# A relational graph layer on one core: eleven tiles of messages fetched row by row instead of 29, a head of 520 tiles, and x for the end loaded in pieces

## The chip, the core and the metric

The kernel runs on one core of one Trainium2 chip. The metric is the device time of one execution in microseconds (us); the time before is the median of three executions.

## The reference

x has 12,500 nodes of 64 features. There are 200,000 edges, each with a source, a destination, one of 64 relations and a weight; the edges are sorted by destination, and low node numbers have many edges. With h = relu(layernorm(x)) the result is:

```python
W   = einsum('rb,bio->rio', comp, basis)              # 64 matrices of 64 x 64
msg = h[src] * norm
s   = segment_sum(msg, etype * N + dst)              # per relation and node
y   = relu(einsum('rni,rio->no', s, W) + bias) + relu(h @ res_w.T + res_b)
out = x + (y - mean(y)) * rsqrt(var(y) + BN_EPS) * gamma + beta   # mean and var over nodes
```

## The kernel before

The edges lie in 1,563 tiles of 128. They are treated in two ways.

**The table.** Since a message times a matrix is linear, the kernel first computes the products of every node with all 64 matrices and writes them to device memory (`z_table`, 205 MB): TensorE (PE) multiplies (L1132), ScalarE (ACT) empties PSUM into `zst` (L578), SyncE (SP) stores 1 MB at a time (L441). When it has landed, the edge tiles from 512 on (1,051 of them) need one row of 64 numbers for each edge. Each such table tile is gathered, then PE multiplies it with a one-hot matrix `oh`, which VectorE (DVE) builds from destinations and weights (L1009), so that one matmul (L1248) adds 128 rows into a window of nodes; four tiles make a unit, and DVE adds its window to `acc` (L991). `s_agg` counts the tiles multiplied.

**The head.** The first `HEAD` = 512 tiles (the nodes with the most edges) don't use the table. GpSimd (POOL) gathers their raw x rows while the table is being written (L528), SP stores them eight tiles at a time to `head_rows`, and later they are read back: DVE and ACT normalize them (L1020 to L1035, L687, L700, L701; L1022 subtracts the means of eight tiles), PE multiplies with a one-hot of (node, relation) (L1040, L1262), DVE adds to `sacc` (L1001), and each of six chunks ends in 32 matmuls with the matrices (L1271, "relations"). The list `sums` spreads the head's items between the table tiles 4 to 855 in a fixed order, which PE, DVE and ACT all follow.

**Who gathers table tiles.** POOL gathers 1,022 of them, one indirect DMA each (L555), into a ring of 36 buffers (`ys`, NY = 36): gather q waits until the tile of gather q - 36 has been multiplied. SP fetches 20 tiles and ACT 9, each as 128 single-row DMAs (`fetch`, L394), into three buffers each. SP takes a tile after each 50 gathers (`SP_EVERY`). `owner` is the table of who fetches what.

**The end.** `acc` holds the sums of node pairs in two halves. The epilogue has 13 chunks of 1,024 nodes (512 columns; the last 128): PE adds the halves (`sum_halves`, L1206), ACT adds the bias and takes the relu (`shifted`, L655), DVE adds the residual part and takes statistics (`moments`, L927, L929). Eleven chunks are done early, between late table tiles (`DONE`, `EPI_EARLY`); chunks 11 and 12 come behind the last tile. Then come the statistics over all nodes (L1061 and on), ACT scales each chunk (L728), PE transposes it back (L1088), DVE adds x (L1082, `xo`, a view of `zst`), SP stores it (L498). `zst` is also where `sacc` lies, so SP loads x only when the relations are through (`s_rel`) and, in program order, when all its rows are fetched: one DMA of 3 MB and one small one (L490, L493).

Of the kernel before, what the change touches and what calls it, by code (L numbers as in the profile page):

```python
# [6 lines left out]
F32 = mybir.dt.float32  # L7
I32 = mybir.dt.int32
# [5 lines left out]
P = 128  # L14
# [3 lines left out]
GT = 8  # L18
# [13 lines left out]
HEAD = 512  # L32
# [3 lines left out]
HEAD_ENDS = (209, 296, 362, 418, 467, HEAD)  # L36
# [10 lines left out]
WINS = (36, 40, 46, 50, 54, 60, 64, 68, 72, 76, 82)  # L47
# [3 lines left out]
DONE, DONE_STEP = ((176, 9), (187, 11)), 5  # L51
# [3 lines left out]
SP_EVERY, SP_FIRST, NSP = 50, 58, 3  # L55
ACT_BATCH, ACT_REST, ACT_EPI, ACT_TILES, NACT = 14, 64, 10, 9, 3
ACT_LATE = 30


def rgcn_kernel(nc, x, src, dst, etype, weight, basis, comp, bias, res_w, res_b, gamma, beta, out):  # L60
# [15 lines left out]
    HR = HEAD // HC  # L76
# [5 lines left out]
    assert LE < UT * P and 2 * UT * P == GE  # L82
    assert 64 < GB <= GA <= P and HEAD % GT == 0 and HEAD % HB == 0 and HR <= P and len(WINS) * WIN_BLOCK == NGZ

# [9 lines left out]

    chunk_of = [sum(t >= end for end in HEAD_ENDS) for t in range(HEAD)]
# [14 lines left out]
    assert epi_after == sorted(epi_after) and epi_after[-1] + NOH + 1 < NZT  # L110
# [29 lines left out]
    tile_at_factor, tile_now = [], 0  # L140
    for kind, t, *_ in sums:
        if kind == "tile":
            tile_now = t
        elif kind == "factor":
            tile_at_factor.append(tile_now)

    def tile_of_row(n):

        if n < ACT_BATCH * NHB:
            return tile_at_factor[n // ACT_BATCH]  # L150
        return HEAD_UNTIL + (n - ACT_BATCH * NHB) * 0.36

    owner, pooled, nsp, nact = {}, 0, 0, 0
    for u, tiles in enumerate(units[:-NU]):
        pooled += len(tiles)
        if u % NU < NU - 1:
            continue
        if nact < ACT_TILES and unit_end[u] >= tile_of_row((nact + 1) * P - 1) + ACT_LATE:
            owner[unit_end[u]] = ("act", nact)
            nact += 1  # L160
            pooled -= 1
        elif pooled >= SP_FIRST + SP_EVERY * nsp:
            owner[unit_end[u]] = ("sp", nsp)
            nsp += 1
            pooled -= 1
    assert nact == ACT_TILES
    tiles_of_queue = {q: [t for t in sorted(owner) if owner[t][0] == q] for q in ("sp", "act")}
    pool_tiles = [t for t in range(NZT) if t not in owner]
    pool_nth = {t: q for q, t in enumerate(pool_tiles)}
    for a in range(NACT, ACT_TILES):  # L170
        assert tiles_of_queue["act"][a - NACT] < tile_of_row(a * P)
# [6 lines left out]
    with ExitStack() as ctx:  # L178
# [25 lines left out]
        def rest(size):  # L204
# [13 lines left out]
        act_rows = fetched[:, NSP * F:(NSP + NACT) * F].rearrange("p (s f) -> p s f", f=F)  # L218
# [4 lines left out]
        xdup = shared[:, 2 * BANK + 2 * LNT * F:4 * BANK + 2 * LNT * F].rearrange("p (s t a f) -> p s t a f", s=2, a=2, f=F)  # L223
        base_h, span_h = (acc[0:1, k * HEAD:(k + 1) * HEAD] for k in range(2))
# [23 lines left out]
        hlo_f, hhi_f = (wgt_all[:, HEAD + k * HC * P:HEAD + (k + 1) * HC * P] for k in range(2))  # L248
        hspan = sb("hspan", [P, 2, HC])
        off_i = sb("off_i", [1, HEAD], I32)  # L250
# [60 lines left out]
        s_act = [sem(f"s_act{k}") for k in range(NACT)]  # L311
# [11 lines left out]
        s_e1, s_eh, s_ey, s_bst, s_st, s_sc, s_o, s_oc, s_out = (  # L323
            sem(n) for n in ("s_e1", "s_eh", "s_ey", "s_bst", "s_st", "s_sc", "s_o", "s_oc", "s_out"))
# [83 lines left out]
        def _(e):  # L408
# [8 lines left out]
            for arr, to in ((dst, dst_i), (src, src_i), (etype, ety_i), (weight, wgt_f)):  # L417
# [3 lines left out]
                e.dma_start(to[64:GB - 1, 1, :], arr[g1 + 64 * GE:(NG - 1) * GE].rearrange("(g n) -> g n", n=GE)).then_inc(s_zin, 16)  # L421
# [5 lines left out]
            def store_head(b):  # L427
                e.wait_ge(s_hg[b % NRING], 16 * HB * (b // NRING + 1))
                e.dma_start(hd[b, :, :], ring[:, b % NRING, :, :].rearrange("p i f -> p (i f)")).then_inc(s_hst[b % NRING], 16)

# [883 lines left out]
```

## Time and profile before

| | |
|---|---|
| time, three executions | 1994.21, 1989.40, 1991.76 us; median 1991.76 |
| the profiled execution | 1994.12 us, of which the span of its instructions is 1992.1 us |
| busy | PE 1604.7 us, POOL 1479.3, ACT 927.1, DVE 923.4 |
| mean granted TensorE clock | 0.729 |

Times are read from the span's start. "x128" at a row's end means 128 instructions merged into one row; a bracket gives the idle time of the engine ahead of the row and what ended it. SPq and ACTq rows are DMA issues of SP and ACT. The time of a POOL gather is the time in which POOL works on it; its data land later.

### The profile page before, as it was taken

What the parts mean: (1) busy time and instruction counts of PE and PEld (TensorE: products, weight loads), DVE (VectorE), ACT (ScalarE), POOL (GpSimd) and SP (SyncE); (2) the same over time, 40 slices, a digit from 0 to 9 for tenths busy, and PEclk for the clock granted to TensorE, in tenths of its full rate; (3) what the DMA queues carried; (4) which work ended last, traced back from release to release, by engine and by line L of the source; (5) the groups of instructions that cost most, each with busy time, mean ns of one, the idle gap of its engine ahead of it and who ended that gap; (6) DMA issues with size and microseconds to landing.
All of it is one profiled execution on the core that took longest, in us unless ns stands there. A gap on an engine that the chain in (4) does not pass through costs nothing. (4 is left out here: it accounts for less than half of the span.)

```text
span 1992.1 us, 36246 instructions
## 1 busy us (share of the span) xinstructions
PE 1604.7 (81%) x6504; PEld 820.8 (41%) x6553; DVE 923.4 (46%) x3200; ACT 927.1 (47%) x2171; POOL 1479.3 (74%) x1548
## 2 busy tenths in 40 slices
PE   4599999999989858988878798888888989845444
PEld 4243444433333335655544453443444434322222
DVE  6631111311100057887846683783856848424223
ACT  4587777777777465555524442452424424000002
POOL 6777777777777677777777777777777777777773
PEclk9999999999999655555566557568667585856556
DMA  9599999999999522222221221221221211111114
GB/s 189 205 401 405 405 406 399 405 405 405 406 401 403 182 43 49 49 55 50 55 39 38 49 49 33 44 55 32 46 44 38 49 33 38 29 27 28 28 27 141
DMA packets 121905, 308.05 MB, mean 155 GB/s; under 512 B 51100, under 2 KB 51319, under 8 KB 96358
## 3 DMA queue, kind: packets, MB, share of 16 engines
q1 hardware_dynamic: 59822, 236.64, 30.4%
q0 software_dynamic: 49088, 50.36, 12.5%
q10 hardware_dynamic: 12768, 18.71, 3.4%
q14 instruction: 169, 1.38, 0.2%
q8 instruction: 58, 0.95, 0.2%
HBM read 79.75 MB, written 225.83 MB: 153 GB/s over the span
## 5 line engine op out<-in xcount | busy, mean ns | idle before, releaser
L555 POOL DMA_INDIRECT shared<-z_table,idx_all x1022 | 982.8, 962 | 320.4 <-issue 237.1
L528 POOL DMA_INDIRECT acc<-in_x,idx_all x512 | 494.3, 965 | 162.8 <-issue 155.8
L1132 PE MATMUL zps<-wp,res 128*128 128x512 bf16 x2303 | 524.4, 382 | 41.6 <-ACT zst L578 28.9
L578 ACT ACTIVATE zst<-zps 128x512 f32<-128x512 f32 (+1 forms) x784 | 411.3, 602 | 149.8 <-DMA z_table<-zst 127.0
L1132 PEld LDWEIGHTS zps<-wp,res 128*128 128x128 bf16 x2352 | 219.0, 98 | 341.3 <-ACT zst L578 99.4
L1262 PE MATMUL mps<-res 128*128 128x160 f32 (+4 forms) x684 | 347.1, 611 | 11.8 <-issue 6.3
L700 ACT ACTIVATE res<-res,hw 128x64 f32<-128x64 f32 x512 | 176.3, 344 | 302.2 <-DVE hw L1035 118.5
L1009 DVE TENSOR_SCALAR shared<-iota,rel_all,wgt_all 128x36 f32<-128x36 f32 (+10 forms) x1051 | 312.5, 324 | 1.1 <-issue 0.9
L1248 PE MATMUL aps<-shared 128*64 128x36 f32 (+10 forms) x1030 | 193.3, 314 | 123.7 <-DVE shared L1009 57.7
L1248 PE MATMUL zps<-shared 128*64 128x36 f32 (+10 forms) x1014 | 188.7, 313 | 98.6 <-DVE shared L1009 40.5
L1248 PEld LDWEIGHTS aps<-shared 128*64 128x64 f32 x1030 | 126.6, 191 | 298.2 <-issue 199.2
L1248 PEld LDWEIGHTS zps<-shared 128*64 128x64 f32 x1014 | 125.4, 192 | 268.6 <-issue 181.2
L803 DVE SCALAR_TENSOR_TENSOR shared<-zps,res 128x512 f32<-128x512 f32 (+1 forms) x25 | 17.0, 678 | 400.5 <-ACT res L607 400.5
L1262 PEld LDWEIGHTS mps<-res 128*128 128x128 f32 x684 | 168.6, 305 | 45.3 <-issue 10.8
L1271 PE MATMUL zps<-zst,res 128*64 128x256 f32 x384 | 179.3, 607 | 0.0
L1040 DVE TENSOR_SCALAR res<-iota,rel_all 128x160 f32<-128x160 f32 (+4 forms) x512 | 172.8, 338 | 0.2 <-issue 0.2
L1262 PE MATMUL zps<-res 128*128 128x160 f32 (+4 forms) x340 | 172.0, 608 | 0.5 <-issue 0.3
L701 ACT ACTIVATE res<-res,hw 128x64 f32<-128x64 f32 x512 | 170.2, 332 | 0.0
L1001 DVE TENSOR_TENSOR zst<-zst,mps 128x160 f32 (+4 forms) x342 | 124.5, 364 | 78.4 <-PE mps L1262 73.2
L661 ACT ACTIVATE zst<-ones 128x2048 f32<-128x2048 f32 x24 | 43.8, 1895 | 152.2 <-PE zps L1271 152.2
L1020 DVE TENSOR_REDUCE hm<-res 128x8 f32<-128x512 f32 x64 | 43.8, 685 | 103.2 <-DMA res<-head_rows 94.4
L1262 PEld LDWEIGHTS zps<-res 128*128 128x128 f32 x340 | 83.8, 305 | 16.7 <-issue 1.0
(152 smaller groups left out, 881.4 us busy)
## 6 DMA issues: line engine op xcount, KB each, us to landing
z_table<-zst SPq DMA_DIRECT2D x194, 1024.0 KB, 9.6
wp<-z_table SPq DMA_DIRECT2D x2560, 0.2 KB
wp<-z_table ACTq DMA_DIRECT2D x1152, 0.2 KB
head_rows<-acc SPq DMA_DIRECT2D x64, 256.0 KB, 9.9
shared<-z_table,idx_all POOLq DMA_INDIRECT x1022, 2.5
res<-head_rows ACTq DMA_DIRECT2D x62, 256.0 KB
acc<-in_x,idx_all POOLq DMA_INDIRECT x512, 6.2
zst<-in_x SPq DMA_DIRECT2D x1, 3072.0 KB
```

The source lines that it names most:

```text
L528: e.indirect_dma_start(out=ring[:, b % NRING, i, :], out_offset=None, in_=x, in_offset=bass.IndirectOffsetOnAxis(ap=idx_all[:, t:t + 1], a ...
L555: e.indirect_dma_start(out=ys[:, q % NY, :], out_offset=None, in_=table[:, :], in_offset=bass.IndirectOffsetOnAxis(ap=idx_all[:, col:col + ...
L578: e.activation(to, frm, ACT.Copy).then_inc(s_ez, 1)
L700: e.activation(ab[:, t % NABS, 0, :], hs[:, n % 2, i, :], ACT.Identity, scale=hw[:, n % 2, i, 0:1])
L701: e.activation(ab[:, t % NABS, 1, :], hs[:, n % 2, i, :], ACT.Identity, scale=hw[:, n % 2, i, 1:2]).then_inc(s_hab, 1)
L1001: e.tensor_tensor(win, win, head_psum(t)[:, 0:w], ALU.add).then_inc(s_hadd, 1)
L1009: e.tensor_scalar(oh[:, t % NOH, 0:w], iota[:, 0:w], rel_all[:, col:col + 1], wgt_all[:, col:col + 1], ALU.is_equal, ALU.mult).then_inc(s_ ...
L1040: e.tensor_scalar(hoh[:, t % NHOH, 0:w], iota[:, 0:w], rel_all[:, t:t + 1], None, ALU.is_equal).then_inc(s_hoh, 1)
L1132: last = e.matmul(to, lhsT=stationary(px, pw), rhs=moving(px, pw), start=(a == 0), stop=(a == 2))
L1248: e.matmul(unit_psum(u)[h:h + F, 0:w], lhsT=rows, rhs=oh[:, t % NOH, 0:w], start=(k < 2), stop=(k >= size - 2)).then_inc(s_agg, 1)
L1262: e.matmul(head_psum(t)[:, 0:w], lhsT=ab[:, t % NABS, :, :].rearrange("p a f -> p (a f)"), rhs=hoh[:, t % NHOH, 0:w], start=True, stop=Tru ...
L1271: last = e.matmul(zps[0:F, NZB - 1, 0:SUM_NODES], lhsT=wf[:, q, :], rhs=by_relation[:, q, :], start=(q == 0), stop=(q == HALF - 1))
```

## The change

- `HEAD` goes from 512 to 520 tiles. Head indices, destinations, types and weights were loaded as 128 rows of four tiles; the eight new tiles (`MAIN` to `HEAD`) come as four more small DMAs (`xsrc_i`, `xdst_i`, ...), issued by ACT at the start, with small copies on DVE and small transposes on PE beside each that was there.
- DVE writes the head's indices to `idx_all` ahead of its first pass over x rather than behind it, and in two parts, so that POOL waits for the first 64 tiles' indices and then, at tile 64, for the rest (`IDX_FROM`).
- ACT fetches no rows. SP fetches a tile after each 80 gathers, the first after 150: by the planner's rule these are the table tiles 151, 231, 311, 399, 479, 559, 639, 719, 799, 879 and 959, eleven in all. POOL's table gathers become 1,043 - 11 = 1,032, its head gathers 520.
- SP waits for the relations (`s_rel`) ahead of its tenth tile, number 879, and issues x for the end in 13 pieces, one after each 16 rows of its last two tiles.
- `DONE` has a third entry: chunk 11 of the epilogue is done after table tile 1,036. Of the last part, POOL scales chunks 3, 6, 9 and 12, and ACT the other nine.
- A few one-hot windows are two columns wider, the head's chunk bounds are moved, and SP loads one row set less for each of four arrays.

```diff
-HEAD = 512
+HEAD, MAIN = 520, 512
-HEAD_ENDS = (209, 296, 362, 418, 467, HEAD)
+HEAD_ENDS = (212, 301, 368, 425, 475, HEAD)
-DONE, DONE_STEP = ((176, 9), (187, 11)), 5
+DONE, DONE_STEP = ((176, 9), (187, 11), (194, 12)), 5
+POOL_SCALES = (3, 6, 9, 12)
-SP_EVERY, SP_FIRST, NSP = 50, 58, 3
-ACT_BATCH, ACT_REST, ACT_EPI, ACT_TILES, NACT = 14, 64, 10, 9, 3
-ACT_LATE = 30
+SP_EVERY, SP_FIRST, NSP = 80, 150, 3
+X_WITH, X_STEP = 2, 16
...
-                for j, t in enumerate(tiles_of_queue["sp"]):
+                loaded = 0
+                for j, t in enumerate(sp_tiles):
                     if j >= NSP:
-                        e.wait_ge(s_agg, tiles_of_queue["sp"][j - NSP] + 1)
+                        e.wait_ge(s_agg, sp_tiles[j - NSP] + 1)
+                    if j == len(sp_tiles) - X_WITH:
+                        e.wait_ge(s_rel, NHK)
                     for r in range(P):
                         fetch(e, regs, t, r, sp_rows[:, j % NSP, :], s_sp[j % NSP])
-                e.wait_ge(s_rel, NHK)
+                        if j >= len(sp_tiles) - X_WITH and r % X_STEP == X_STEP - 1 and loaded < NEPI:
+                            load_x(loaded)
+                            loaded += 1
...
-            e.wait_ge(s_hidx, 1)
             for t in range(HEAD):
+                if t in IDX_FROM:
+                    e.wait_ge(s_hidx, IDX_FROM.index(t) + 1)
...
+            e.wait_ge(s_st, 9)
+            for n in POOL_SCALES:
+                y = acc[:, n * EPI:n * EPI + epi_width[n]]
+                e.tensor_scalar(y, y, bmv[:, 6:7], bmv[:, 8:9], ALU.mult, ALU.add).then_inc(s_scp, 1)
...
+            e.dma_start(xsrc_i[:, :], extra_rows(src)).then_inc(s_hsrc, 16)
...
+            for to, arr in ((xdst_i, dst), (xety_i, etype), (xlo_f, weight)):
+                e.dma_start(to[0:EX, :], extra_rows(arr)).then_inc(s_hin, 16)
...
-                            fetch_rows(ACT_BATCH * (i + 1) // HB - ACT_BATCH * i // HB)
...
-                fetch_rows(ACT_REST)
                 for n in range(EPI_EARLY):
-                    if n == done_from[1]:
-                        fetch_rows(ACT_TILES * P)
                     shifted(n)
-                    fetch_rows(ACT_EPI)
...
+            e.wait_ge(s_hrow, 1)
+            take_main(idx_all, 0, IDX_FROM[1] // HC).then_inc(s_hidx, 1)
+            take_main(idx_all, IDX_FROM[1] // HC, HR)
+            e.tensor_copy(idx_all[:, MAIN:HEAD], mflat[:, HC * P:HC * P + EX]).then_inc(s_hidx, 1)
```

In the rows below, which give the program's order and no times, a line's number is that of its own version. The first place is the start of ACT's queue, before:

```order
L564 DMA idx_all<-in_src 128x512
L565 DMA comp_sb<-in_L_gnn_comp 64x64
L566 DMA resw_sb<-in_L_gnn_res_w 64x64
L567 DMA resw_sb<-in_L_gnn_res_w 64x64
L568 DMA res<-in_L_gnn_basis 64x4096
L569 DMA rel_all<-in_dst 128x512
L570 DMA rel_all<-in_edge_type 128x512
L571 DMA wgt_all<-in_edge_weight 128x512
```

and with the change:

```order
L563 DMA idx_all<-in_src 128x512
L564 DMA xsrc_i<-in_src 8x128
L565 DMA comp_sb<-in_L_gnn_comp 64x64
L566 DMA resw_sb<-in_L_gnn_res_w 64x64
L567 DMA resw_sb<-in_L_gnn_res_w 64x64
L568 DMA res<-in_L_gnn_basis 64x4096
L569 DMA rel_all<-in_dst 128x512
L570 DMA rel_all<-in_edge_type 128x512
L571 DMA wgt_all<-in_edge_weight 128x512
L573 DMA acc<-in_dst 8x128
L573 DMA acc<-in_edge_type 8x128
L573 DMA acc<-in_edge_weight 8x128
```

One small load (`xsrc_i`) now stands ahead of the loads of comp, res_w and basis, and three more ahead of the biases and of all that ACT computes.

The second place is PE behind the last table tiles (L1248 and L1246 are those tiles, into banks `aps` and `zps`; L1206 and L1208 are `sum_halves`), before:

```order
L1248 MATMUL zps<-shared 64x82 x8
L1248 MATMUL aps<-shared 64x82 x8
L1248 MATMUL zps<-shared 64x82 x7
L1248 MATMUL zps<-shared,wp 64x82
L1248 MATMUL aps<-shared 64x82 x8
L1248 MATMUL zps<-shared 64x82 x3
L1226 UNCONDITIONAL_BRANCH
L1206 MATMUL mps<-acc,stack 64x512 x2
L1206 MATMUL zps<-acc,stack 64x128 x2
```

and with the change:

```order
L1246 MATMUL zps<-shared 64x82 x8
L1246 MATMUL aps<-shared 64x82 x8
L1246 MATMUL zps<-shared 64x82 x5
L1208 MATMUL mps<-acc,stack 64x512 x2
L1246 MATMUL zps<-shared 64x82 x3
L1246 MATMUL aps<-shared 64x82 x3
L1228 UNCONDITIONAL_BRANCH
L1208 MATMUL zps<-acc,stack 64x128 x2
```

The 512-column chunk has moved from behind the last tile to six tiles ahead of it; only the 128-column one is left behind.

The third place is SP's queue where it loads x for the end (`zst<-in_x`), before, behind its last row:

```order
L394 DMA wp<-z_table 1x64
L393 ISA
L394 DMA wp<-z_table 1x64
L467 UNCONDITIONAL_BRANCH
L490 DMA zst<-in_x 128x12x512
L493 DMA zst<-in_x 106x128
L498 DMA out_x<-zst 128x512 x12
```

and with the change, the first of 13 such places, inside tile 879:

```order
L379 DMA wp<-z_table 1x64
L378 ISA
L379 DMA wp<-z_table 1x64
L437 DMA zst<-in_x 128x512
L378 ISA
L379 DMA wp<-z_table 1x64
L378 ISA
```

The load is cut into pieces that stand between rows of the table, the last of them 80 rows into SP's last tile.

## Rows read from the trace of the kernel before

**Rows 1.** The page, part 2: busy tenths of POOL and of DMA in 40 slices.
```profile
POOL 6777777777777677777777777777777777777773
...
DMA  9599999999999522222221221221221211111114
```

**Rows 2.** The page, parts 5 and 6: the two gathers, and issue to landing.
```profile
L555 POOL DMA_INDIRECT shared<-z_table,idx_all x1022 | 982.8, 962 | 320.4 <-issue 237.1
L528 POOL DMA_INDIRECT acc<-in_x,idx_all x512 | 494.3, 965 | 162.8 <-issue 155.8
...
shared<-z_table,idx_all POOLq DMA_INDIRECT x1022, 2.5
```

**Rows 3.** Waits of POOL: engine, line, releaser, us in total, times, longest.
```profile
POOL shared L555 <- issue: 237.1, 777, 0.3
```

**Rows 4.** Timeline of POOL: the first and the last gather from the table.
```profile
668.85 0.94 POOL L555 DMA_INDIRECT shared<-z_table,idx_all  x1 [8.87 <-DMA z_table<-zst]
...
1962.27 0.94 POOL L555 DMA_INDIRECT shared<-z_table,idx_all  x1 [0.30 <-issue]
```

**Rows 5.** POOL in three stretches, the gathers of L555 alone.
```profile
669.00:694.00 25.00, 18.91 (x21) 0.50 0.27 65
860.00:940.00 80.00, 60.93 (x63) 0.50 0.23 51
...
1900.00:1950.00 50.00, 37.81 (x41) 0.51 0.15 27
```

**Rows 6.** Timeline of a stretched gather, 969 to 971 us.
```profile
969.26 0.69 DVE L1022 TENSOR_TENSOR res<-res,hm 128x512 f32<-128x512 f32 x1
...
969.53 1.23 POOL L555 DMA_INDIRECT shared<-z_table,idx_all  x1 [0.30 <-issue]
```

**Rows 7.** Timeline of the DMA queue of SP from 1829 us.
```profile
1829.09 127.33 SPq L394 DMA_DIRECT2D wp<-z_table  x257
1956.79 0.41 SPq L490 DMA_DIRECT2D zst<-in_x  x1
```

**Rows 8.** Timeline behind the last gather: its landing, the last two chunks.
```profile
1968.33 0.54 PE L1248 MATMUL zps<-shared 128*64 128x82 f32 x2 [0.59 <-DMA shared<-z_table,idx_all]
...
1969.35 2.08 PE L1206 MATMUL mps<-acc,stack 128*64 128x512 f32 x4 [0.48 <-DVEq L1055]
...
1971.48 0.69 ACT L655 ACTIVATE acc<-mps,cols 128x512 f32<-128x512 f32 x1 [73.81 <-PE mps L1206]
1972.07 0.36 ACT L655 ACTIVATE acc<-zps,cols 128x128 f32<-128x128 f32 x1
...
1974.15 0.51 DVE L1061 BATCH_NORM_AGGREGATE halves<-bst 128x2 f32<-128x78 f32 x1
```

**Rows 9.** Timeline of the last stretch: DVE adds x to chunks 4 to 12.
```profile
1982.57 5.18 DVE L1082 TENSOR_TENSOR zst<-zst,zps 128x512 f32<-128x512 f32 x9 [0.17 <-PE zps L1088]
```

**Rows 10.** Timeline of the start, and where the stream of products begins.
```profile
4.40 0.45 ACTq L570 DMA_DIRECT2D rel_all<-in_edge_type  x1
...
9.92 1.10 POOL L528 DMA_INDIRECT acc<-in_x,idx_all  x1 [6.97 <-DVE idx_all L746]
...
12.95 0.22 DVE L793 TENSOR_TENSOR shared<-zps,wp 128x64 f32<-128x64 f32 x1 [3.32 <-ACT wp L607]
...
59.17 1.94 PE L1088 MATMUL zps<-ident,shared 128*128 128x128 f32 x8 [13.90 <-DVE shared L773]
```

**Rows 11.** DMA from 60 to 660 us: queue 0, and the gathers issued.
```profile
q0 software_dynamic: 15079, 15.47, 8.5%
...
acc<-in_x,idx_all POOLq DMA_INDIRECT x474, 6.2
```

**Rows 12.** Timeline of PE, the end of the head: relations, then a table tile.
```profile
1731.66 1.02 PE L1271 MATMUL zps<-zst,res 128*64 128x256 f32 x2
...
1736.83 0.50 PE L1248 MATMUL zps<-shared 128*64 128x72 f32 x2 [0.53 <-DMA shared<-z_table,idx_all]
```

**Rows 13.** Timeline of POOL at the start: an operation on 288 columns.
```profile
2.48 0.38 POOL L518 IOTA iota<- 128x288 f32 x1
```

More of the change, by code:

```diff
@@ L109, in rgcn_kernel @@
                  for k in range(len(DONE)) for n in range(done_from[k + 1] - done_from[k])]
-    assert epi_after == sorted(epi_after) and epi_after[-1] + NOH + 1 < NZT
+    moments_at = [min(t + NOH + 1, NZT - 1) for t in epi_after]
+    assert epi_after == sorted(epi_after) and epi_after[-1] < NZT and len(set(moments_at)) == EPI_EARLY
     epi_run = [2 * w // P for w in epi_width]
@@ L137, in rgcn_kernel @@
     assert done == len(head_items)
[L140 to L153, printed above, removed]
+    owner, pooled, nsp = {}, 0, 0
     for u, tiles in enumerate(units[:-NU]):
         pooled += len(tiles)
[L156 to L163, printed above, removed]
+        if u % NU == NU - 1 and pooled >= SP_FIRST + SP_EVERY * nsp:
+            owner[unit_end[u]] = nsp
             nsp += 1
             pooled -= 1
[L166 to L167 removed]
+    sp_tiles = sorted(owner)
     pool_tiles = [t for t in range(NZT) if t not in owner]
     pool_nth = {t: q for q, t in enumerate(pool_tiles)}
[L170 to L171 removed]
     table = nc.dram_tensor("z_table", [NCLS * N * CLS, F], F32)
@@ L429, in store_head @@
                 e.dma_start(hd[b, :, :], ring[:, b % NRING, :, :].rearrange("p i f -> p (i f)")).then_inc(s_hst[b % NRING], 16)
+            regs = [e.alloc_register(f"sp_row{k}") for k in range(REGS)]
             stored = 0
@@ L466, in _ @@
                 e.wait_ge(s_sum, 1)
+                for n in range(NEPI):
+                    load_x(n)
             with e.Else():
@@ L669, in _ @@
                     clear(sacc[:, a:a + 2048]).then_inc(s_flush, 1)
-                e.wait_ge(s_met, 3)
-                regs = [e.alloc_register(f"act_row{k}") for k in range(REGS)]
-                fetched_rows = [0]
-                def fetch_rows(count):
-                    for n in range(fetched_rows[0], min(fetched_rows[0] + count, ACT_TILES * P)):
-                        a, r = divmod(n, P)
-                        if r == 0 and a >= NACT:
-                            e.wait_ge(s_agg, tiles_of_queue["act"][a - NACT] + 1)
-                        fetch(e, regs, tiles_of_queue["act"][a], r, act_rows[:, a % NACT, :], s_act[a % NACT])
-                        fetched_rows[0] = n + 1
                 for kind, n, *_ in sums:
@@ L1282, in _ @@
             for n, w in enumerate(epi_width):
-                e.wait_ge(s_sc, n + 1)
+                pools = sum(k <= n for k in POOL_SCALES)
+                if n in POOL_SCALES:
+                    e.wait_ge(s_scp, pools)
+                else:
+                    e.wait_ge(s_sc, n + 1 - pools)
                 if n >= NZB:
```

141 lines of the change are left out of this document (75 added, 66 removed).

## The prediction

> **What bounds the kernel now.** I read the slices of the page first. POOL shows 7 in nearly every slice from the second to the last but one, while DMA is full in the first third alone [rows 1]. An engine that is 70 to 79% busy all the time may be waiting a little each time or may be full. The groups settle it: 512 head gathers take 494.3 us of work and 162.8 us of gaps, 1,022 table gathers 982.8 and 320.4 [rows 2], and the waits put 237.1 us of those gaps down to "issue", 777 times and never more than 0.3 us [rows 3]. A gather of 0.94 us is followed by a gap of 0.30 [rows 4], also in the 25 us when neither SP nor ACT fetches anything: 18.91 busy of 25.00 is 75.6%, or 0.94 of 1.25 [rows 5]. So POOL issues at its own pace from 9.92 us [rows 10] to 1962.27 us [rows 4], with one real wait, 8.87 us for the table to land [rows 4]. PE is busier in sum, but it is ahead where it counts: when the head's relations end at 1732.7 us it needs 4 us until it waits for a gather's data [rows 12]. The time is POOL's start, its gathers, that one wait, and the tail behind the last gather.
>
> The pace is 1.270 us in the head ((494.3 + 155.8) / 512, without the 7.0 us ahead of the first) and 1.267 at the table ((982.8 + 320.4 - 8.9) / 1022) [rows 2, 4]. The unhindered pace is 1.248, so 1,022 gathers lose 19 us to stretching. What stretches them is seen in one pair of rows: DVE starts L1022, a subtraction with two SBUF inputs, at 969.26 for 0.69 us, and the gather that starts at 969.53 takes 1.23 us instead of 0.94 [rows 6]. From 1900 to 1950 us, with SP fetching rows without a pause [rows 7] and no L1022, the share is 75.6% again; from 860 to 940, with L1022 at work, it is 76.2% [rows 5]. The rows that SP and ACT fetch don't slow POOL; DVE does.
>
> By the Trainium skill (SBUF — State Buffer, section SBUF: two separate sides) DVE and GpSimd share a port pair that the first to start holds for its whole instruction, and a DVE operation with two SBUF inputs takes it against a GpSimd operation that reads SBUF. By that rule, the trace agrees: the stretched gather ends about when it would if it had begun behind L1022. It also says that SP's own DMAs don't take part in this, so by it their removal gives POOL nothing.
>
> **Start.** ACT issues one more DMA ahead of res_w and basis and three more ahead of the biases. Issues follow each other by 0.45 us and a little [rows 10], so four cost 4 x 0.49 = 2.0 us, and all of ACT's work begins 2.0 later. DVE stood 3.32 us waiting for ACT at 12.95 [rows 10], so it is late by the same; the two go on in turns, and PE waits 13.90 us for DVE's product at 59.17, where the stream begins [rows 10]. I take the whole 2.0 as the delay of the stream; the bounds are 0 (all of it absorbed in between) and 2.6. On the other side POOL starts earlier, since its indices are copied ahead of DVE's three operations on x: near 6.8 instead of 9.92.
>
> **The stream and the table's landing.** DMA is at 0.99 there [rows 1], so the stream is as long as its bytes take. Gathers are 8.5% of 16 engines in 600 us, for 474 of them [rows 11]: 0.108 us each, 0.8 for eight more. The table lands 2.0 + 0.8 = 2.8 later, and POOL's first table gather moves from 668.85 to 671.6 (bounds 669 to 673).
>
> **Eight more head gathers** cost 8 x 1.270 = 10.2 us, but they lie in what was the 8.87 us wait: 6.8 + 520 x 1.270 = 667.2, before 671.6. They are free. If POOL started no earlier they would end at 670.3, still before.
>
> **Ten more table gathers** (1,032 for 1,022) have no cover: POOL has no other gap. 10 x 1.267 = **12.7 us** (12.5 at the unhindered pace). The head has one block of eight more, one L1022 more, 0.3 us, which I leave in the range. The last gather starts at 671.6 + 1,031 x 1.267 = 1977.9 instead of 1962.27; I take 2.8 + 12.7 = 15.5 later, 1977.8.
>
> **The tail.** Behind the last gather stand 29.8 us (1962.27 to 1992.1).
> - The last gather's data reached PE at 1968.33, 6.1 us on [rows 8], where 2.5 is the median [rows 2]; SP had issued the 3 MB of x at 1956.79 [rows 7]. With x loaded in pieces 100 us earlier this is 2.5: -3.5 us. Bounds: 0, if something else delayed it, and -3.6.
> - Chunk 11 is no longer behind the last tile. PE's passes begin at 1969.35, ACT's relu of chunk 11 runs at 1971.48, of chunk 12 at 1972.07, and the statistics begin at 1974.15: 4.8 us [rows 8]. With only the 128-column chunk I count 0.75 (PE) + 0.4 (ACT) + 0.6 (DVE's two small operations) + 0.1 = 1.9: -2.9 us (bounds -2.2 to -3.3). Ahead of the last tiles the chunk costs PE 2.08 us, with six gathers or 7.5 us still to come, and these six tiles need 6 x 0.5 [rows 12]: hidden, with some 2 us to spare.
> - POOL's share of the scaling gives nothing. From chunk 4 on DVE works with 0.17 us of idle time ahead, nine chunks in 5.18 us [rows 9]; it, and PE before it, set the pace, not ACT. Does it cost? No row shows this POOL operation. The nearest is 0.38 us for 288 columns [rows 13], so 0.7 for 512 in proportion; the other end is four times that, 2.8. Chunk 3 is wanted three ACT steps of 0.7 in, and then one each 2.1 or more: below 2.1 it is free, at 2.8 the fourth would be 2 to 3 us late. I take 0, being near the lower row.
>
> By the Trainium skill (GPSIMD Engine Reference, section 3.1) a simple one-input operation runs at about 1.03 cycles per element; by it the sum stays as it is.
>
> **Hidden, and what if not.** The rows that SP and ACT no longer issue stood in queues that nobody at the bound waits for. SP's tile 879 is a new risk: its rows are issued only when the relations are through. In the old order that is 1732.7; now I expect 1740 (the 2.8, and eight head tiles more for PE). SP takes 127.33 / 257 = 0.495 us for a row [rows 7], so 128 rows and eight loads of 0.41 take 66.7 us: data at 1807. PE wants this tile when its neighbours land, near 1775, so PE stands for some 30 us. POOL isn't stopped: gather 906 is the first that needs a tile behind 879, it starts at 671.6 + 906 x 1.267 = 1819.5, 12 us later. SP's last tile is in by 1872, wanted at 1876.
>
> **Sum.** 2.8 + 12.7 - 3.5 - 2.9 + 0 = **+9.1 us**. Against the profiled execution: 1994.1 + 9.1 = 2003.2. The median of the runs lies 2.4 below the profiled one, so I forecast 1991.8 + 9.1 = **2000.9 us**, slower by 0.46%. Its own range, from the bounds: 0 to 3.5 at the start, 12.5 to 13.5, -5.8 to -7 in the tail (with -2.2 if the load wasn't to blame), 0 to 2.5 for the scaling, and 3 either way for how DVE's operations happen to meet the gathers: 1995 to 2008.
>
> **Rivals.**
> - *Faster: the stretching goes.* Without ACT's fetches its factors come on time and L1022 falls elsewhere in POOL's cycle. If all 19 us went, the sum would be -10, 1982 us; it decides from 9.1 of 19.3 on, about half. For it: the hits depend on phase. Against it: 65 blocks remain, and row fetches show no effect [rows 5].
> - *Slower still: POOL stops behind tile 879.* Every microsecond that the relations end after 1752 goes to POOL. If they end 20 late, at 1760, it is 8 us, giving 2009. For it: the order of the wait; against it: 12 us of margin.
> - *About the same.* The start's delay is absorbed (-2.8) and fewer gathers are stretched (-3 or more): +3, 1995.
> - *The load of x wasn't what delayed the last data.* Then 3.5 come back: 2004.4, inside the forecast's range.
>
> **Chances.** Forecast with its own range 0.68, stretching goes 0.09, POOL stops 0.08, about the same 0.15. The range of 1992 to 2008.5 leaves out the two outer cases. A measurement of this kernel tells about 0.2% (4 us) from no change: faster by more 0.10, within it 0.16, slower by more 0.74.
>
> **What would show it.** Right: POOL's first head gather before 8 us; its wait for the table 4 to 5 us instead of 8.87, and the first table gather at 671 to 673; 1,032 gathers at 1.267; the last data 2.5 us behind the last gather; PE idle for 25 to 35 us at tile 879 while POOL's waits stay at 0.3. Wrong: a POOL pace under 1.258, a POOL wait of microseconds near 1819, a table that lands before 669.5, or chunks 6, 9 and 12 waiting for POOL.

## The result, and the profile after

The changed kernel takes 2000.73 us in the median of 5 runs (2000.44 to 2004.86), the kernel before, run beside it, 1992.28 us (1989.4 to 1994.21). The ratio is 1.0049, with a 95% interval of 1.0034 to 1.0063: slower by about half a per cent. The forecast was 2000.9 us. The profiled execution of the changed kernel took 2000.53 us with a span of 1998.4, against 1994.1 and 1992.1 before. So the two profiles differ by 6.4 us and the medians by 8.5: the profiled execution of the kernel before lies about 2 us above its median, that of the changed kernel 0.2 below its own.

The lines that answer to [rows 1] and [rows 2], from the page of the changed kernel (L546 is the gather from the table, L519 that of the head):

```profile
POOL 6777777777777777777777777777777777777774
...
DMA  9599999999999522222211221221211211122112
...
L546 POOL DMA_INDIRECT shared<-z_table,idx_all x1032 | 988.7, 958 | 316.1 <-issue 248.1
L519 POOL DMA_INDIRECT acc<-in_x,idx_all x520 | 503.6, 968 | 163.0 <-issue 157.9
```

POOL is the bound as before: 7 in every slice between the ends. What changed is the last digit of DMA, 4 before and 2 now: the 3 MB of x are no longer loaded in the last slice. A table gather is 958 ns on the mean instead of 962, which is less stretching than before; the forecast had it in its range, not in its sum.

The start of the stream of products against [rows 10], then POOL's timeline where the head's gathers end and the table's begin, and at its last gather, against [rows 4]:

```profile
60.78 1.94 PE L1089 MATMUL zps<-ident,shared 128*128 128x128 f32 x8 [13.86 <-DVE shared L770]
...
7.79 1.14 POOL L519 DMA_INDIRECT acc<-in_x,idx_all  x1 [4.84 <-DVE idx_all L733]
...
668.61 0.95 POOL L519 DMA_INDIRECT acc<-in_x,idx_all  x1 [0.30 <-issue]
671.36 0.94 POOL L546 DMA_INDIRECT shared<-z_table,idx_all  x1 [1.80 <-DMA z_table<-zst]
...
1973.34 0.94 POOL L546 DMA_INDIRECT shared<-z_table,idx_all  x1 [0.30 <-issue]
```

The first table gather is 2.5 us later than before and the last one 11.1. Between them are 1,031 steps in 1301.98 us: a pace of 1.263 instead of 1.267. The wait for the table is down to 1.80 us, from 8.87: the eight more head gathers fill nearly all of it.

The tail, against [rows 8] and [rows 9]:

```profile
1970.60 1.21 PE L1208 MATMUL mps<-acc,stack 128*64 128x512 f32 x2
1971.87 0.69 ACT L657 ACTIVATE acc<-mps,cols 128x512 f32<-128x512 f32 x1 [64.75 <-PE mps L1208]
...
1975.86 0.54 PE L1246 MATMUL aps<-shared 128*64 128x82 f32 x2 [0.72 <-DMA shared<-z_table,idx_all]
...
1976.88 0.69 PE L1208 MATMUL zps<-acc,stack 128*64 128x128 f32 x4 [0.48 <-DVEq L1056]
...
1978.65 0.51 DVE L1062 BATCH_NORM_AGGREGATE halves<-bst 128x2 f32<-128x78 f32 x1
1979.21 0.59 PE L1278 MATMUL mps<-halves,wmean 128*128 128x2 f32 x2 [1.64 <-DVE halves L1062]
...
1982.05 6.45 ACT L714 ACTIVATE acc<-acc,bmv 128x512 f32<-128x512 f32 x9 [0.81 <-DVE bmv L1078]
1982.12 2.70 POOL L553 TENSOR_SCALAR acc<-acc,bmv 128x512 f32<-128x512 f32 x4 [7.84 <-DVE bmv L1078]
...
1984.86 9.14 SPq L488 DMA_DIRECT2D out_x<-zst  x13
...
1987.48 5.22 DVE L1083 TENSOR_TENSOR zst<-zst,zps 128x512 f32<-128x512 f32 x9 [0.17 <-PE zps L1089]
```

The last gather's data reach PE 2.5 us behind its start (6.1 before). Chunk 11 passes PE and ACT while gathers are still running, and from the last chunk's pass (1976.88) to the statistics (1978.65) it is 1.8 us instead of 4.8. DVE's nine adds still follow each other with 0.17 us between, 5.22 us against 5.18: relieving ACT by POOL speeds nothing up.

Behind the last gather stand 25.1 us, against 29.8.

### The profile page after: what moved, and what is told of

Read it like the earlier page. It is cut to its first block and busy times, and to the rows that moved or that the text cites. A ratio compares the mean times of both kernels' runs of the same rounds, so it can differ in the third digit from the quotient of the medians.

```text
span 1998.4 us, 29426 instructions
## 1 busy us (share of the span) xinstructions
PE 1633.6 (82%) x6559; PEld 820.3 (41%) x6559; DVE 929.6 (47%) x3234; ACT 902.4 (45%) x2186; POOL 1497.1 (75%) x1570
## 3 DMA queue, kind: packets, MB, share of 16 engines
q0 software_dynamic: 49664, 50.96, 12.7%
## 5 line engine op out<-in xcount | busy, mean ns | idle before, releaser
L546 POOL DMA_INDIRECT shared<-z_table,idx_all x1032 | 988.7, 958 | 316.1 <-issue 248.1
L519 POOL DMA_INDIRECT acc<-in_x,idx_all x520 | 503.6, 968 | 163.0 <-issue 157.9
L1133 PE MATMUL zps<-wp,res 128*128 128x512 bf16 x2352 | 531.9, 382 | 35.2 <-ACT zst L580 26.4
L1246 PE MATMUL aps<-shared 128*64 128x36 f32 (+10 forms) x1040 | 206.8, 314 | 126.0 <-DMA shared<-z_table,idx_all 66.0
L1246 PE MATMUL zps<-shared 128*64 128x36 f32 (+10 forms) x1024 | 204.9, 312 | 107.9 <-DMA shared<-z_table,idx_all 63.2
L1246 PEld LDWEIGHTS aps<-shared 128*64 128x64 f32 x1040 | 133.1, 191 | 323.6 <-issue 154.3
L1246 PEld LDWEIGHTS zps<-shared 128*64 128x64 f32 x1024 | 130.7, 188 | 314.3 <-DMA shared<-z_table,idx_all 154.2
L1269 PE MATMUL zps<-zst,res 128*64 128x256 f32 x384 | 189.1, 611 | 0.0
L992 DVE TENSOR_TENSOR acc<-acc,zps 128x36 f32 (+10 forms) x130 | 28.8, 222 | 142.9 <-PE zps L1246 111.1
L677 ACT ACTIVATE res<-res 128x512 f32<-128x512 f32 x65 | 40.9, 629 | 114.6 <-DVE res L1023 114.1
```

The source lines that it names most:

```text
L519: e.indirect_dma_start(out=ring[:, b % NRING, i, :], out_offset=None, in_=x, in_offset=bass.IndirectOffsetOnAxis(ap=idx_all[:, t:t + 1], a ...
L546: e.indirect_dma_start(out=ys[:, q % NY, :], out_offset=None, in_=table[:, :], in_offset=bass.IndirectOffsetOnAxis(ap=idx_all[:, col:col + ...
L1133: last = e.matmul(to, lhsT=stationary(px, pw), rhs=moving(px, pw), start=(a == 0), stop=(a == 2))
L1246: e.matmul(unit_psum(u)[h:h + F, 0:w], lhsT=rows, rhs=oh[:, t % NOH, 0:w], start=(k < 2), stop=(k >= size - 2)).then_inc(s_agg, 1)
L1269: last = e.matmul(zps[0:F, NZB - 1, 0:SUM_NODES], lhsT=wf[:, q, :], rhs=by_relation[:, q, :], start=(q == 0), stop=(q == HALF - 1))
```

## The experiments

Twelve kernels ran, four at a time on three chips, each four with runs of the kernel before on the same chip. In the first it took 1994.41 us (median of 21), in the second 1994.19 (15), in the third **3092.94** (11). The third chip is a case of its own, and comes last.

**1. How much do the table gathers cost, and do row fetches stretch them?** The kernel before, with nothing but its fetched tiles reduced to eleven, so 1,040 table gathers:

```diff
-SP_EVERY, SP_FIRST, NSP = 50, 58, 3
-ACT_BATCH, ACT_REST, ACT_EPI, ACT_TILES, NACT = 14, 64, 10, 9, 3
+SP_EVERY, SP_FIRST, NSP = 80, 150, 3
+ACT_BATCH, ACT_REST, ACT_EPI, ACT_TILES, NACT = 14, 64, 10, 0, 3
```

> The kernel before with only the table of who fetches changed: SP fetches the same 11 tiles as in the changed kernel, ACT none, so POOL gathers 1,040 table tiles instead of 1,022. Nothing else is different: head of 512, x loaded at the end of SP's list. My theory (POOL's issue pace is all that counts, 1.263 to 1.267 us a gather): +18 x 1.265 = +22.8 us in the gathers. SP is now done with its rows some 70 us before the end, so the 3 MB of x no longer meets the last gather: -3.5. Sum +19.3, a ratio of 1.0097 (1.008 to 1.011). Rival (fetched rows stretch the gathers, so that fewer of them give the time back): the pace falls to 1.248, -19, sum 0, ratio near 1.000.

Measured: 2011.85 us (5 runs), ratio 1.0085 [1.0071, 1.0099], 17.4 us for 18 gathers. Its page and its end:

```profile
L555 POOL DMA_INDIRECT shared<-z_table,idx_all x1040 | 999.5, 961 | 324.0 <-issue 258.1
```
```profile
1984.87 0.94 POOL L555 DMA_INDIRECT shared<-z_table,idx_all  x1 [0.30 <-issue]
```

The mean of 961 ns is that of before (962): without ACT's 1,152 fetches and 1,152 of SP's the gathers are as stretched as with them. 18 gathers at the pace of 1.266 are 22.8 us. The last one's data reached PE 2.7 us behind it instead of 6.25, which gives 3.5 back; SP had issued the load of x at 1744.75 us and not at 1956.79 [rows 7]. The profiles are 19.6 us apart, and the ratio lies in the expected range.

**2. The changed kernel with 20 of SP's tiles (`SP_EVERY, SP_FIRST = 50, 58`), so 1,023 table gathers.**

> The changed kernel with SP fetching a tile after each 50 gathers again, 20 tiles, ACT none: POOL gathers 1,023 table tiles instead of 1,032. My theory: -9 x 1.263 = -11.4 us against the changed kernel, so -2.9 us against the kernel before (2000.7 - 11.4 = 1989.3, ratio 0.9985; 0.997 to 1.000). Rival (the last rows of SP come too late, since SP needs 61 us a tile and has 63): PE waits for SP at the last tile, 1031, and gives 3 to 8 us back.

Measured: 1992.29 us (11 runs), ratio 0.9989 [0.998, 0.9998]. Nine gathers are gone, but SP's last tile is now late; the timeline of PE at the end:

```profile
1967.00 0.40 PE L1246 MATMUL aps<-shared,wp 128*64 128x82 f32 x1 [14.28 <-DMA wp<-z_table]
```

PE stands 14.28 us for a tile from SP, while the last gather had started at 1963.43; the tail is 30.6 us instead of 25.1. The ratio lies in the theory's range, but partly by luck: against the changed kernel the medians are 8 us apart and not 11.4, and the profile shows what the rival named, 5.5 us given back behind the last gather (this execution, 1995.84 us, was the slowest of the eleven). So the fetched tiles pay as long as SP gets through them before the end.

**3. The changed kernel once more, beside the next three on one chip.**

> The changed kernel as it is, to stand beside the other kernels of this call on the same chip. Expected: 1.0049 of the kernel before again, its pace at the table 1.263 to 1.267 us for one gather, and a tail of 25 us behind the last gather.

Measured: 2000.25 us (5 runs), ratio 1.0037 [1.0024, 1.0051]; gathers of 958 ns, pace 1.2624, a tail of 24.9 us.

**4. x loaded whole and late.**

```diff
-                        if j >= len(sp_tiles) - X_WITH and r % X_STEP == X_STEP - 1 and loaded < NEPI:
-                            load_x(loaded)
-                            loaded += 1
-                assert loaded == NEPI
+                e.wait_ge(s_agg, NZT - 7)
+                whole, run = (NEPI - 1) * EPI, epi_run[0]
+                e.dma_start(xoflat[:, 0:whole // P * F].rearrange("p (c r) -> p c r", c=NEPI - 1),
+                            x[0:whole, :].rearrange("(c i j) f -> i c (j f)", c=NEPI - 1, j=run)).then_inc(s_xre, 16 * (NEPI - 1))
+                load_x(NEPI - 1)
```

> The changed kernel with one thing undone: x for the end is loaded in one DMA of 3 MB, and only when seven table tiles are left to sum, so that it runs beside the last gathers, as before the change. Theory (the load of x delayed the last gather's data before): the landing behind the last gather goes from 2.7 us back to about 6, and the time is 3.5 us longer than that of the changed kernel. Rival (something else delayed it, and the load is hidden): the landing stays at 2.7 us and the time is the same.

Measured: 2007.39 us (5 runs), ratio 1.0067 [1.0053, 1.0081]. Its timeline, SP's load and the last gathers (L547) and their products (L1247):

```profile
1968.90 0.43 SPq L482 DMA_DIRECT2D zst<-in_x  x1
...
1974.59 0.94 POOL L547 DMA_INDIRECT shared<-z_table,idx_all  x1 [0.30 <-issue]
1976.63 0.80 PE L1247 MATMUL zps<-shared 128*64 128x82 f32 x4 [3.74 <-DMA shared<-z_table,idx_all]
...
1980.68 0.53 PE L1247 MATMUL aps<-shared 128*64 128x82 f32 x2 [0.40 <-DMA shared<-z_table,idx_all]
```

From the last gather to its product it is 6.1 us again, and to the last of its two products 6.28 against 2.67 in experiment 3: 3.6 us, the theory's number for the landing. The time is another matter: 3.5 us were expected and the medians are 7.1 apart. In the profiles, 5.4 apart, the last gather itself starts 1.8 us later (1974.59 against 1972.78), of which the first table gather's later start is 1.1. What lies beyond the tail's 3.7 isn't explained by the load, and was not looked into by a run.

**5. Chunk 11 late again** (`DONE` without its third entry, `(194, 12)`).

> The changed kernel with chunk 11 of the epilogue behind the last tile again (two entries in DONE). My theory: +2.9 us against the changed kernel (ratio to before 1.0057), seen as 4.8 us instead of 1.8 from the first matmul of sum_halves to the statistics in the profile. Rival (the early chunk costs PE as much ahead of the last tiles as it saves behind): 0.

Measured: 2000.6 us (6 runs), ratio 1.0033 [1.002, 1.0045]. Its last stretch:

```profile
1980.64 0.51 DVE L1062 BATCH_NORM_AGGREGATE halves<-bst 128x2 f32<-128x78 f32 x1
...
1986.12 1.47 DVE L1083 TENSOR_TENSOR zst<-zst,zps 128x512 f32<-128x512 f32 x2 [2.12 <-PE zps L1089]
1986.84 8.13 SPq L488 DMA_DIRECT2D out_x<-zst  x13
1987.76 6.35 DVE L1083 TENSOR_TENSOR zst<-zst,zps 128x512 f32<-128x512 f32 x11 [0.17 <-PE zps L1089]
```

From the last gather's last product to the statistics it is 5.6 us (1975.01 to 1980.64) instead of 2.6 (1976.05 to 1978.65 in the changed kernel): the term of 3 us is there. But the whole tail is 26.2 us, only 1.2 longer than the 25.1 and 1.3 than the 24.9 of the two profiles of the changed kernel. Two things give 1.8 back here. PE's granted clock goes to full at 1988.1 us, 2.0 us behind DVE's first add, and in the changed kernel at 1988.0, 3.9 us behind it. So only one step from add to add takes 0.85 us here and the rest soon 0.60, where the changed kernel has three or four of 0.85; that is 0.6. And the output ends 4.2 us behind the start of SP's last issue, not 5.1; with what SP's queue loses ahead of it that is the other 1.2, and its cause is open (experiment 6). In time the run can't be told from the changed kernel: of the 2.9 us expected none shows.

**6. All scaling by ACT** (`POOL_SCALES = ()`).

> The changed kernel with all 13 chunks scaled by ACT, as before; POOL does nothing behind its last gather. My theory (DVE's additions of x and PE set the pace, not the scaling): no change against the changed kernel, ratio to before 1.004 to 1.005. Rival A (POOL's share gives what it was to give): 1 to 2.5 us slower than the changed kernel, 1.0055. Rival B (POOL at work is why SP's last four issues took 0.5 to 0.66 us instead of 0.33 and the output landed 1.3 us later than the tail's sum has it): 1.3 us faster, 1.0036, and SP's issues at 0.33 to the end.

Measured: 1999.3 us (10 runs), ratio 1.0022 [1.0013, 1.0032], below all three expected ratios. Its last stretch:

```profile
1985.59 8.96 ACT L714 ACTIVATE acc<-acc,bmv 128x512 f32<-128x512 f32 x13 [0.81 <-DVE bmv L1078]
...
1988.39 8.45 SPq L488 DMA_DIRECT2D out_x<-zst  x13
...
1991.02 5.07 DVE L1083 TENSOR_TENSOR zst<-zst,zps 128x512 f32<-128x512 f32 x9 [0.17 <-PE zps L1089]
```

ACT now scales for 8.96 us instead of 6.45, and DVE's nine adds take 5.07: ACT was never the bound. The tail behind the last gather is 23.6 us against 25.1 and 24.9. The difference lies at the very end: SP's 13 issues take 8.45 us instead of 9.14 and 9.05, and the output ends 4.2 us behind the start of the last of them instead of 5.1. Of the nine profiles with POOL's scaling five end so (5.1 us behind the last issue) and four don't (4.1 to 4.3: experiments 5, 8, 9 and 10); of the five without it none does (4.1 to 4.3). So in some profiles POOL's scaling goes with a cost of up to 1.4 us, and with no gain in any. That the scaling is the cause isn't shown, and in time the difference isn't clear of noise: experiment 5, on the same chip and with POOL's scaling, has a ratio of 1.0033 with an interval that overlaps this one.

**7. The subtraction in eight operations**, each with one SBUF input and a number per partition:

```diff
-                        e.tensor_tensor(rows, rows, hm[:, b % 2, 0, :].unsqueeze(2).broadcast_to([P, HB, F]),
-                                        ALU.subtract).then_inc(s_hc, 1)
+                        for i in range(HB):
+                            last = e.tensor_scalar(rows[:, i, :], rows[:, i, :], hm[:, b % 2, 0, i:i + 1], None, ALU.subtract)
+                        last.then_inc(s_hc, 1)
```

> The changed kernel with the subtraction of 8 tiles that has two SBUF inputs written as 8 operations of one tile with one SBUF input and a number per partition. Theory (this subtraction stretches the gathers that it meets): no gather is stretched by it any more, the pace goes from 1.263 to about 1.255 us, and the time falls by 8 us (0.4%). Rival (any DVE work stretches them, or the stretching has another source): eight operations meet more gathers than one, the pace stays or rises, and the time is the same or longer.

Measured: 1995.17 us (11 runs), ratio 1.0009 [1.0, 1.0018]. From its page and timeline:

```profile
L546 POOL DMA_INDIRECT shared<-z_table,idx_all x1032 | 982.8, 952 | 316.2 <-issue 243.6
...
L519 POOL DMA_INDIRECT acc<-in_x,idx_all x520 | 502.7, 967 | 163.1 <-issue 158.2
```
```profile
999.86 0.94 POOL L546 DMA_INDIRECT shared<-z_table,idx_all  x1 [0.30 <-PE aps L1247]
...
1000.09 1.40 DVE L1024 TENSOR_SCALAR res<-res,hm 128x64 f32<-128x64 f32 x8
1001.10 0.95 POOL L546 DMA_INDIRECT shared<-z_table,idx_all  x1 [0.30 <-PE aps L1247]
```

Eight operations take 1.40 us of DVE where one took 0.69, they are still running when the gather of 1001.10 starts, and that gather takes 0.95, not the 1.23 of [rows 6]. The mean falls from 958 to 952 ns, the pace to 1.2572, and the medians by 5.1 us. The theory holds for the subtraction, and its size was guessed too high: 8 expected, 5 measured. Some 10 us of stretching remain, 1,032 times 952 less 943 ns. No run separates their sources, but the traces show which DVE operation was running when each gather started:

| gathers that start during | experiment 3 | experiment 7 |
|---|---|---|
| the subtraction | 30, mean 1,236 ns, 8.8 us over 943 ns | 67, mean 959 ns, 1.0 us |
| the head's one-hots (one SBUF input) | 110, mean 976 ns, 3.6 us | 90, mean 996 ns, 4.8 us |
| the residual's addition in `moments`, 128x512 | 5, mean 1,058 ns, 0.6 us | 9, mean 1,169 ns, 2.0 us |
| no DVE operation | 466, 0.2 us | 410, 0.2 us |

So the stretching belongs to DVE's operations. The eight small ones remove the subtraction's part, and the others' part is somewhat larger in this profile. The third chip's profiles agree: 5 to 6 us of stretching with the eight operations (experiments 10 to 12), 14 with the one (experiment 9).

**8. ACT fetches nine tiles again, SP nineteen**, in the changed kernel (the planner's code for ACT's tiles as before the change, `SP_EVERY, SP_FIRST, NSP = 50, 58, 3`), so 1,015 table gathers.

> The changed kernel, but 28 tiles fetched row by row instead of 12: 9 by ScalarE as before the change and 19 by SyncE, one each 50 gathers. POOL is left with 1,015 table gathers instead of 1,032. Theory (each table gather costs its pace, nothing else does): 17 x 1.263 = 21.5 us less than the changed kernel, 0.6% below the kernel before. Rival (the fetches of ScalarE cost what they save, by stretching or by late factors): the time is that of the changed kernel less 5 us or less.

Measured: **1978.62 us** (5 runs, 1978.19 to 1982.33), ratio 0.9931 [0.9917, 0.9944]: faster than both kernels. From its page and POOL's timeline (L573 is the table gather):

```profile
L573 POOL DMA_INDIRECT shared<-z_table,idx_all x1015 | 973.5, 959 | 309.5 <-issue 230.0
```
```profile
670.64 0.94 POOL L546 DMA_INDIRECT acc<-in_x,idx_all  x1 [0.30 <-issue]
671.89 0.95 POOL L573 DMA_INDIRECT shared<-z_table,idx_all  x1 [0.30 <-issue]
...
1953.67 0.94 POOL L573 DMA_INDIRECT shared<-z_table,idx_all  x1 [0.30 <-issue]
```

(The changed kernel fetches 11 tiles row by row, not the 12 of the expectation; the 17 gathers are right.) The last gather starts 19.1 us sooner than in experiment 3, the tail is 1.8 shorter, and the median 21.6 lower. That this meets the expected 21.5 so closely is partly luck: 17 gathers at the pace are 21.5, the first table gather starts 0.6 later and the pace is 1.7 us longer in sum, and the tail's 1.8, a matter of the clock and of the output's end (experiments 5 and 6), fills the gap. 959 ns with 3,584 row fetches, 958 with 1,408: no stretching by the fetches shows. There is no wait for the table at all here, 0.30 us like any gap, so the 520 head gathers are at least as long as what they hide behind; a 521st would cost.

**9 to 12. On the third chip.** These were to measure the start's delay and to add up what had helped. The chip answered another question.

The changed kernel with its three small head loads issued by SyncE:

> The changed kernel, but the three small loads of the head's eight extra tiles (nodes, relations, weights) are issued by SyncE instead of ScalarE. Theory (ScalarE's added DMA issues delayed the start, and through it the table): ScalarE starts 1.5 us sooner, the table lands 1.5 us sooner, but POOL's head gathers end at 668.7 to 669.6 and hold the first table gather at 669 to 670 instead of 671.3; the time falls by 1 to 1.5 us. Rival (the start's delay was absorbed, the table's landing is late for another reason, such as the bytes of eight more gathers): the first table gather stays at 671.3 us and the time is the same.

Experiment 8 with the eight subtractions of 7:

> The changed kernel with 28 tiles fetched row by row (ScalarE 9, SyncE 19) and the subtraction of 8 tiles written as 8 operations with one SBUF input. Theory (both gains add: 17 gathers at their pace, and the stretching by the subtraction): 21.5 + 5.5 = 27 us below the changed kernel, 1.2% under that, 0.9875 of the kernel before. Rival (with more row fetches the eight operations come at worse moments, or PE or DVE becomes the bound): 0.991 or more.

The same with all scaling by ACT:

> The kernel with 28 tiles fetched row by row and eight subtractions, and POOL's four chunks of the final scaling given back to ScalarE. Theory (POOL's scaling shortens nothing and slows the last DMA issues): the tail behind the last gather is 23.6 us instead of 25, the time up to 1.4 us shorter than that of its pair with POOL's scaling. Rival (POOL's scaling relieves ScalarE): the time is longer by 1 us or more.

The same with the small loads on SyncE too:

> The kernel with 28 tiles fetched row by row, eight subtractions and scaling by ScalarE alone, and also the three small loads of the extra head tiles issued by SyncE. Theory (ScalarE's issues at the start delay the table): the first table gather starts 1 to 1.5 us sooner than without this, and the time is shorter by as much: 0.986 of the kernel before. Rival (absorbed): the same time as without it.

Measured, beside 3092.94 us for the kernel before: 2597.57 (6 runs), ratio **0.8427** [0.839, 0.8464]; 3025.49, ratio 0.9823 [0.9772, 0.9875]; 3032.29, 0.9833 [0.9786, 0.988]; 3028.14, 0.9805 [0.9764, 0.9846]. The last three can't be told apart, so on what they were to show they are inconclusive. The first says that on this chip a kernel with 11 fetched tiles takes 16% less than the one with 29. The kernel before has no profile here, but experiment 10 has one, with 28 fetched tiles. SP's queue, first in experiment 8 on its chip, then in experiment 10 on this one:

```profile
1264.34 135.86 SPq L405 DMA_DIRECT2D wp<-z_table  x280
```
```profile
1420.42 218.84 SPq L405 DMA_DIRECT2D wp<-z_table  x269
```

A fetched row takes 0.485 us there and 0.814 in this stretch (0.74 to 0.87 from tile to tile). 128 rows are 62 us or 104, and SP has a tile to deliver each 50 gathers, or 63 us. So SP is behind from its first tiles on and everybody waits for it, as the page and POOL's waits of experiment 10 show:

```profile
L1295 PE MATMUL aps<-shared,wp 128*64 128x70 f32 (+7 forms) x28 | 6.8, 345 | 378.9 <-DMA wp<-z_table 378.9
```
```profile
POOL shared L573 <- PE zps L1295: 398.0, 102, 37.6
POOL shared L573 <- PE aps L1295: 344.6, 97, 36.3
```

PE waits for SP's rows, and POOL's gathers, whose buffers PE frees, wait for PE: 743 us of stops of up to 37.6 us. The kernel with 11 tiles (experiment 9) has 101 us from tile to tile. Its rows are slower still (0.89 to 1.12 us in all tiles but one, up to 143 us for a tile), but PE waits for them only four times, 125.6 us in all. One of these is what the prediction had as a rival:

```profile
L1247 PE MATMUL zps<-shared,wp 128*64 128x78 f32 x2 | 0.5, 364 | 71.9 <-DMA wp<-z_table 71.9
```
```profile
POOL shared L549 <- PE aps L1247: 183.4, 85, 50.4
```

PE stands 71.9 us for tile 879, and this time POOL stops behind it, for 50.4. In the changed kernel on its own chip the same tile cost PE 28.4 us and POOL nothing (next section). POOL's stops of more than 3 us add up to 116 us in experiment 9; another 200 us or so go in small waits, which PE's four waits for SP don't explain. The stream is slower too, mostly 235 to 305 GB/s in its slices instead of 404, and the first table gather starts at 946 to 960 us. Why this chip is slow wasn't found. In experiment 10 the median distance from one row to the next is 0.417 us, as in experiment 8 (0.416); but 39% of the distances are 0.6 us or more, against 6%, and in the slow ones SP stands 0.7 us, once or several times, between two instructions that follow each other at once in experiment 8.

The start can still be read here, since the first 20 us are as on the other chips. ACT's DMA issues and its first work, of the changed kernel, then of experiment 9:

```profile
6.18 0.36 ACTq L573 DMA_DIRECT2D acc<-in_dst  x1
6.57 0.31 ACTq L573 DMA_DIRECT2D acc<-in_edge_type  x1
6.91 0.31 ACTq L573 DMA_DIRECT2D acc<-in_edge_weight  x1
...
13.59 0.22 ACT L580 ACTIVATE compT<-zps 64x64 f32<-64x64 f32 x1
```
```profile
12.37 0.22 ACT L581 ACTIVATE compT<-zps 64x64 f32<-64x64 f32 x1
```

Three issues fewer are 1.2 us between these two, and 1.0 to 1.1 among the profiles of the third chip (13.47 and 13.48 in experiments 10 and 11, 12.37 and 12.49 in 9 and 12), where 1.5 was expected; four more in the changed kernel were 1.8 (11.76 before). Whether the table's landing follows by as much was not measured on a chip where it counts.

## Why the prediction was right, and where it wasn't

The sum was +9.1 us; the profiles give +6.4 and the medians +8.5. The mechanism is the one forecast: ten gathers more at POOL's pace, less what the tail gives back. That 2000.73 lies within 0.2 us of 2000.9 is luck, as the terms show:

- **Start and table, +2.8: +2.5.** ACT's work begins 1.8 us later (2.0 forecast), the stream of products 1.6 (60.78 against 59.17), the first table gather 2.5 (671.36 against 668.85). This is the before-and-after comparison alone: in the seven other profiles of the new head on the first chips the first table gather starts between 670.7 and 673.7 us, in the other one of the old head at 669.7, and the run that should have confirmed the term fell on the third chip.
- **Eight head gathers, free: yes, but barely.** POOL started at 7.8 us, not at 6.8, and the pace of the head was 1.273 us, not 1.270. The last of them ends at 669.6, and the wait is 1.80 us where 4 to 5 were forecast. Experiment 8 had no wait left.
- **Ten table gathers, +12.7: 12.7 at the pace of before, less 4.1.** 1,031 steps at 1.2628 are 4.1 us shorter than at 1.2668. That is the mis-sized term: the stretching, which was carried over at 19 us, is 15.5 here. Experiments 1 and 8 together say that it isn't the fetches (961 ns with few of them, 959 with many). The difference lies in the subtraction: before the change 35 gathers that started during one of its 64 runs took over 1.05 us, after it 23 (of 65 runs); together they lie 11.8 and 8.2 us over 943 ns. Whether that belongs to the change isn't shown. Seven profiles of kernels with the new head and the one subtraction have 13 to 19 us of stretching on the first two chips, the two with the old head both 19; and the 19 among the seven is experiment 6, whose kernel is the changed one up to its last stretch. So one execution differs from another by as much as this term. Experiment 7 shows the subtraction's share by removing it: 5 us.
- **Landing of the last data, -3.5: -3.5**, and experiment 4 brings it back by putting the load back.
- **Chunk 11 early, -2.9: -3.0** at the statistics. In experiment 5 only 1.2 to 1.3 of it reach the end: 0.6 go because the clock's rise doesn't move with the earlier statistics, and 1.2 at the output's end, for a reason that is open.
- **Scaling, 0: a cost.** The tail has 1.8 us more behind the statistics than before: 0.4 up to the first add, 1.4 at the end of the output (5.99 us behind the start of DVE's last add, against 4.60). The first isn't the change's: experiment 1, with the old tail, has the same 5.49 us from the statistics to the first add, where the profile of before has 5.08. The second stands only in profiles with POOL's scaling, in five of nine (experiment 6). POOL needs 0.77 us for a chunk of 512 columns (2.70 for the four, of which the last has 128) and starts them 0.75 apart: near the lower bound of 0.7, and on time. What price there was lay in the output's DMAs, where the prediction looked for none.

What these make: 2.5 + 12.7 - 4.1 - 3.5 - 3.0 + 1.8 = +6.4. The term missed by 4.1 and the one missed by 1.8 cancel in part and, with the 0.3 of the start, leave the sum 2.7 too high; the profile of before, 2 us above its median, hides most of that in the medians.

**Tile 879** went as forecast. The timeline of PE and the waits of POOL in the changed kernel:

```profile
1735.16 6.49 SPq L379 DMA_DIRECT2D wp<-z_table  x16
...
1799.96 0.39 PE L1246 MATMUL zps<-shared,wp 128*64 128x78 f32 x1 [28.42 <-DMA wp<-z_table]
```
```profile
POOL shared L546 <- PE aps L1246: 33.2, 109, 0.3
```

PE stands 28.4 us (25 to 35 forecast), and POOL never more than 0.3: its gather 906 starts at 1815, 15 us behind the data. That margin is a property of how fast SP fetches and of when the relations end: in experiment 9 the tile's 128 rows took 93 us instead of 64, and they began 45 us ahead of when POOL was ready for gather 906 instead of 80, so that the margin of 15 became a stop of 50.

**The rivals.** That all the stretching goes: refuted, 15.5 of 19 remain, and experiment 1 shows that taking the fetches away takes none of it. That POOL stops: not in the measurement of the result nor on the next two chips, and for 50 us on the third. *About the same*: half of it came, the fewer stretched gathers (-4.1), and the other half, a start whose delay is absorbed, did not (+2.5). That the load wasn't to blame: refuted by experiment 4.

By the Trainium skill (SBUF — State Buffer, section SBUF: two separate sides) DVE takes the pair of ports that it shares with GpSimd only with two SBUF inputs, or in a faster mode. The two-input subtraction agrees: gathers that start during it take 1,236 ns in experiment 3, and during the eight short operations of experiment 7, with one SBUF input and twice the time in all, 959. But one SBUF input alone doesn't keep the gathers free: those that start during the head's one-hots, of 160 to 288 columns, take 976 and 996 ns on the mean and up to 1,177. Which mode these run in no run here tells.

## What to carry to other kernels

When one engine issues at a fixed pace from start to end, count its instructions: moving 17 table gathers to idle queues was worth 21.6 us (19.1 of them by the start of the last gather), while every edit of the tail was worth 1 to 4 in the profiles. Work that is handed to a second queue has a rate of its own: write down what it must deliver per unit of the bound's pace (here 62 us of SP's time for each 63 of POOL's) and how much slower the queue may get before the bound waits for it, for a margin of 1 us in 63 is none on another chip. And before an early chunk or a helper engine is counted as a gain, look at what runs behind it: of 3 us won at the statistics 1.2 arrived in the profile and none that could be told in the medians.

## What the hardware showed that wasn't expected

- The same kernel took 1992 to 1994 us in the first measurement and on two chips, and 3093 us on another. SP's row fetches took 0.485 us and 0.72 to 1.12, the stream moved 404 GB/s and some 285, while a gather took 0.96 us on both (957 and 958 ns). Which of two kernels is faster turned with it: the one with 11 fetched tiles is 0.4 to 0.5% slower than the one with 29 on those, and, but for three small loads, 16% faster on this one.
- In the tail PE's granted clock rises within the output stage. In the changed kernel:

```profile
1975.00:1980.00 5.00, 2.16 (x11) 1.38 (x10) 1.31 (x4) 0.37 (x1) 0.00 (x0) 0.50 0.04 7
1980.00:1985.00 5.00, 2.31 (x12) 2.22 (x12) 2.04 (x10) 3.15 (x6) 2.70 (x4) 0.50 0.00 0
1985.00:1990.00 5.00, 5.00 (x35) 5.00 (x33) 4.44 (x7) 3.50 (x5) 0.00 (x0) 0.70 0.76 278
```

  The columns are the stretch, its length, busy us of PE, PE's weight loads, DVE, ACT and POOL, PE's clock, the share of DMA and GB/s. PE was 43 to 46% busy ahead of 1985 at 0.50 (1.2 GHz), and while it rose DVE's adds came each 0.85 us, then each 0.60. The rise came behind the second step in experiments 5 and 8 and up to three steps later elsewhere, and each step (0.85 less 0.60) is 0.25 us of the end.
- A tensor_scalar of 128x512 on GpSimd took 0.77 us, little more than DVE's 0.69 for a two-input operation of that shape.
